# Recurrent layer: the four gates in three PSUM banks, two separate products, and the next chunk's normalisation one step later

## What is computed

```
x_proj = x @ W_ih.T + b_ih + b_hh
for every step t:
    gates = x_proj[t] + h @ W_hh.T
    i, f, g, o = split(gates, 4)
    c = sigmoid(f) * c + sigmoid(i) * tanh(g)
    h = sigmoid(o) * tanh(c)
```

## Time and profile before

| | us |
|---|---|
| median of 3 runs | 5656.29 (5656.06 to 5662.14) |
| the profiled execution's own time | 5652.6 |
| its span | 5650.8 |
| first step of the recurrent layer (AB) | at 4040.4 |
| last HT of the recurrent layer | at 5552.3 |
| VectorE's and the stores' tail behind it | 98 |
| TensorE busy, whole span | 4365.2 (77%) |
| VectorE busy, whole span | 3937.5 (70%) |
| ScalarE busy, whole span | 2516.5 (45%) |
| raw input transfer, issue to landing, median | 1.8 |

### The profile page before, as it was taken

One profiled execution on the slowest core, in us unless ns is written; L12 is line 12 of the kernel. 1 busy time (PEld: TensorE's weight loads), 2 busy tenths in 40 slices (PEclk: granted clock), 3 DMA queues, 4 the chain that ended last, 5 costly groups with the idle time before them and its releaser, 6 DMA issues. The chain is left out here.

```text
span 5650.8 us, 151689 instructions
## 1 busy us (share of the span) xinstructions
PE 4365.2 (77%) x55153; PEld 2972.8 (53%) x55295; DVE 3937.5 (70%) x9254; ACT 2516.5 (45%) x6434; POOL 1642.0 (29%) x1316
## 2 busy tenths in 40 slices
PE   6887888884888888888888868888487777777772
PEld 3444444442455555555555556666376666666662
DVE  5887888783777777777777758888365555555555
ACT  4666666662454555555455524444132323233330
POOL 4767676762223232332323211111000000000000
PEclk9999999996899999999999979999799999999996
DMA  2111111111000000000000023332211111111105
GB/s 58 46 60 46 60 45 60 50 52 41 16 16 21 17 19 19 19 19 15 22 15 19 16 71 105 105 104 93 49 26 26 26 26 24 27 24 27 26 23 124
DMA packets 322638, 233.54 MB, mean 41 GB/s; under 512 B 170381, under 2 KB 288525, under 8 KB 322061
## 3 DMA queue, kind: packets, MB, share of 16 engines
q1 hardware_dynamic: 288268, 217.37, 13.2%
q10 hardware_dynamic: 33792, 8.39, 0.7%
HBM read 158.55 MB, written 67.11 MB: 40 GB/s over the span
## 5 line engine op out<-in xcount | busy, mean ns | idle before, releaser
L2181 PE MATMUL lstm_G_psum<-lstm_Whh,lstm_HT 128*32 128x192 f32 x8192 | 447.2, 336 | 324.4 <-DVE lstm_HT L2353 281.4
L1398 PE MATMUL ssm_J_psum<-ssm_XT,ssm_W_in 128*128 128x512 f32 x1152 | 589.8, 637 | 104.0 <-DVE ssm_CV L1806 102.5
L538 ACT ACTIVATE g_relu<-g_Z_psum 128x512 f32<-128x512 f32 x640 | 380.2, 594 | 598.9 <-PE g_Z_psum L420 598.7
L706 DVE CUSTOM_DVE_ANT_0 g_S<-g_Z_psum,g_relu 128x512 f32<-128x512 f32 x640 | 437.8, 684 | 247.2 <-ACT g_relu L538 237.2
L427 PE MATMUL g_PT_psum<-g_ident,g_PR 128*128 128x128 f32 x2560 | 401.8, 280 | 239.7 <-DVE g_PT L714 164.0
L427 PEld LDWEIGHTS g_PT_psum<-g_ident,g_PR 128*128 128x128 f32 x2560 | 303.5, 143 | 439.2 <-issue 171.3
L547 ACT ACTIVATE g_PR<-g_S,g_nmax 128x512 f32<-128x512 f32 x640 | 460.0, 719 | 107.7 <-DVE g_nmax L706 103.2
L2247 ACT ACTIVATE lstm_TC<-lstm_G_psum 128x192 f32<-128x192 f32 x512 | 170.2, 332 | 749.3 <-PE lstm_G_psum L2181 749.3
L2173 PE MATMUL lstm_G_psum<-lstm_Wih,lstm_XT 128*32 128x192 f32 x8192 | 434.9, 330 | 0.0
L2476 POOL TENSOR_SCALAR lstm_rstd<-lstm_mv 128x4 f32<-128x4 f32 x32 | 7.2, 226 | 1470.2 <-DVE lstm_mv L2336 1470.2
L2181 PEld LDWEIGHTS lstm_G_psum<-lstm_Whh,lstm_HT 128*32 128x32 f32 x8192 | 216.9, 110 | 412.4 <-DVE lstm_HT L2353 333.8
(11 more groups left out here) (256 smaller groups left out, 10550.3 us busy)
## 6 DMA issues: line engine op xcount, KB each, us to landing
g_ADJ<-in_adj SPq DMA_DIRECT2D x64, 1024.0 KB, 6.1
x<-g_XO SPq DMA_DIRECT2D x64, 512.0 KB, 3.4
g_X<-in_x SPq DMA_DIRECT2D x32, 512.0 KB, 5.9
ssm_X<-x SPq DMA_DIRECT2D x32, 512.0 KB, 3.8
x<-ssm_OUT SPq DMA_DIRECT2D x32, 512.0 KB, 2.8
g_X<-x SPq DMA_DIRECT2D x32, 512.0 KB, 3.9
lstm_raw<-x SPq DMA_DIRECT2D x1024, 16.0 KB, 1.8
lstm_U<-x SPq DMA_DIRECT2D x128, 128.0 KB, 3.3
```

The lines of the kernel that those rows point to most:

```text
L538: act.activation(relu[n % 4][:, :], Zb[n % 2][:, :], ACT.Relu, scale=(1.0 - ALPHA) / ALPHA).then_inc(s["relu"], 1)
L706: v.tensor_tensor_reduce(S[n % 4][:, :], Zb[n % 2][:, :], relu[n % 4][:, :], -1.0, 3e38, ALU.add, ALU.min, nmax[:, n % 4:n % 4 + 1]).then_ ...
L1398: ins = pe.matmul(Jb[k % 2][:, :], W_in[:, kc, c:c + P], XT[:, kc, :], start=(kc == 0), stop=(kc == KC - 1))
L2181: ins = pe.matmul(bank[32 * j:32 * (j + 1), 0:last - first], HT[t % 2][:, 32 * kc:32 * (kc + 1)], Whh[:, kc, j, first:last], start=False, ...
```

## The change

Gates move from two pairs of banks to four banks: Gb[0] and Gb[1] hold i and g (128 columns), Fb holds f, Ob holds o, the last two without a second buffer. The weights and the bias are laid out in the order i, g, f, o (PLACE). ScalarE takes three tanh per step (i and g; f; o). VectorE computes IG = (i + 1) * g and FC = (f + 1) * c in two instructions of 64 elements and the cell goes to a tile of its own. The waits for the tiles' and banks' readers follow that. ScalarE's normalisation of the next chunk stands behind `cell` in steps 9 and 10 instead of 8 and 9. In VectorE's side work the second half's four passes go from steps 12 to 15 to steps 13 to 16, step 16 being step 0 of the chunk after.

```diff
+    PLACE = (0, 2, 1, 3)
...
-        TC = [m.sb(f"TC{k}", [P, 4, HB]) for k in range(2)]
+        TIG = [m.sb(f"TIG{k}", [P, 2, HB]) for k in range(2)]
+        TF = [m.sb(f"TF{k}", [P, HB]) for k in range(2)]
+        C = [m.sb(f"C{k}", [P, HB]) for k in range(2)]
...
-        AB = m.sb("AB", [P, 2, HB])
+        IG = m.sb("IG", [P, HB])
+        FC = m.sb("FC", [P, HB])
...
-        Ob = [m.ps(f"O{k}") for k in range(2)]
+        Fb = m.ps("F")
+        Ob = m.ps("O")
...
             def inputs(c, t):
...
-                for bank, first, last, read in ((Gb[t % 2], 0, IFG, s["tg"]), (Ob[t % 2], IFG, 4 * HB, s["to"])):
-                    c.wait(pe, read, S, t - 1)
+                for bank, first, last, read, back in ((Gb[t % 2], 0, 2 * HB, s["tg"], 2), (Fb, 2 * HB, 3 * HB, s["tf"], 1),
+                                                      (Ob, 3 * HB, 4 * HB, s["to"], 1)):
+                    c.wait(pe, read, S, t + 1 - back)
...
             def hidden(c, t):
                 c.wait(pe, s["ht"], S, t + 1)
-                for bank, first, last, made in ((Gb[t % 2], 0, IFG, s["g"]), (Ob[t % 2], IFG, 4 * HB, s["go"])):
+                for bank, first, last, made in ((Gb[t % 2], 0, 2 * HB, s["g"]), (Fb, 2 * HB, 3 * HB, s["gf"]),
+                                                (Ob, 3 * HB, 4 * HB, s["go"])):
...
             def gates(c, t):
                 c.wait(act, s["g"], S, t + 1)
-                c.wait(act, s["ab"], S, t - 1)
-                act.activation(TC[t % 2][:, 0:3, :].rearrange("p g e -> p (g e)"), Gb[t % 2][:, 0:IFG], ACT.Tanh
+                c.wait(act, s["ig"], S, t - 1)
+                act.activation(TIG[t % 2][:, :, :].rearrange("p g e -> p (g e)"), Gb[t % 2][:, 0:2 * HB], ACT.Tanh
                                ).then_inc(s["tg"], 1)
+                c.wait(act, s["gf"], S, t + 1)
+                c.wait(act, s["fc"], S, t - 1)
+                act.activation(TF[t % 2][:, :], Fb[:, 0:HB], ACT.Tanh).then_inc(s["tf"], 1)
+
+            def output_gate(c, t):
                 c.wait(act, s["go"], S, t + 1)
                 c.wait(act, s["h"], S, t - 1)
-                act.activation(TO[t % 2][:, :], Ob[t % 2][:, 0:HB], ACT.Tanh).then_inc(s["to"], 1)
+                act.activation(TO[t % 2][:, :], Ob[:, 0:HB], ACT.Tanh).then_inc(s["to"], 1)
...
                     gates(c, t)
+                    output_gate(c, t)
                     cell(c, t)
-                    if nxt and t in (8, 9):
-                        normalised(c + 1, 2 * (t - 8))
-                        normalised(c + 1, 2 * (t - 8) + 1)
+                    if nxt and t in (9, 10):
+                        normalised(c + 1, 2 * (t - 9))
+                        normalised(c + 1, 2 * (t - 9) + 1)
...
             def step(c, t):
                 c.wait(v, s["tg"], S, t + 1)
                 c.wait(v, s["c2"], S, t)
-                v.scalar_tensor_tensor(out=AB[:, :, :], in0=TC[t % 2][:, 0:2, :], scalar=1.0, in1=TC[t % 2][:, 2:4, :],
-                                       op0=ALU.add, op1=ALU.mult).then_inc(s["ab"], 1)
-                c.wait(v, s["ab"], S, t + 1)
-                v.scalar_tensor_tensor(out=TC[(t + 1) % 2][:, 3, :], in0=AB[:, 1, :], scalar=0.5, in1=AB[:, 0, :],
+                v.scalar_tensor_tensor(out=IG[:, :], in0=TIG[t % 2][:, 0, :], scalar=1.0, in1=TIG[t % 2][:, 1, :],
+                                       op0=ALU.add, op1=ALU.mult).then_inc(s["ig"], 1)
+                c.wait(v, s["tf"], S, t + 1)
+                v.scalar_tensor_tensor(out=FC[:, :], in0=TF[t % 2][:, :], scalar=1.0, in1=C[t % 2][:, :],
+                                       op0=ALU.add, op1=ALU.mult).then_inc(s["fc"], 1)
+                c.wait(v, s["fc"], S, t + 1)
+                v.scalar_tensor_tensor(out=C[(t + 1) % 2][:, :], in0=FC[:, :], scalar=0.5, in1=IG[:, :],
                                        op0=ALU.mult, op1=ALU.add).then_inc(s["c2"], 1)
...
                 if t == 12:
                     counted(c, 14)
                     counted(c, 15)
+                if t == 13:
                     before_it(c, 1)
-                if t == 13:
+                if t == 14:
                     before_added(c, 1)
-                if t == 14:
+                if t == 15:
                     up_to_it(c, 1)
-                if t == 15:
+                if t == S:
                     up_to_taken(c, 1)
...
                     step(c, t)
+                    if prev2 and t == 0:
+                        beside(c + -2, S)
```

More of the change, by code:

```diff
@@ L2015, in lstm_phase @@
     HALF = S // 2
-    IFG = 3 * HB
+    PLACE = (0, 2, 1, 3)
     with ExitStack() as ctx:
@@ L2055, in lstm_phase @@
         REP_AT = 2 * S
-        names = ("w setup_v setup_pe wready zero raw_in st mv rstd shift0 shift xn xt_pe xt g go tg to ab c2 tc h ht lgp lg "
+        names = ("w setup_v setup_pe wready zero raw_in st mv rstd shift0 shift xn xt_pe xt g gf go tg tf to ig fc c2 tc h ht lgp lg "
                  "gate repp gs inc part u done tot bias1 bias2 fin outs").split()
@@ L2245, in gates @@
                 c.wait(act, s["g"], S, t + 1)
-                c.wait(act, s["ab"], S, t - 1)
-                act.activation(TC[t % 2][:, 0:3, :].rearrange("p g e -> p (g e)"), Gb[t % 2][:, 0:IFG], ACT.Tanh
+                c.wait(act, s["ig"], S, t - 1)
+                act.activation(TIG[t % 2][:, :, :].rearrange("p g e -> p (g e)"), Gb[t % 2][:, 0:2 * HB], ACT.Tanh
                                ).then_inc(s["tg"], 1)
+                c.wait(act, s["gf"], S, t + 1)
+                c.wait(act, s["fc"], S, t - 1)
+                act.activation(TF[t % 2][:, :], Fb[:, 0:HB], ACT.Tanh).then_inc(s["tf"], 1)
+            def output_gate(c, t):
                 c.wait(act, s["go"], S, t + 1)
                 c.wait(act, s["h"], S, t - 1)
-                act.activation(TO[t % 2][:, :], Ob[t % 2][:, 0:HB], ACT.Tanh).then_inc(s["to"], 1)
+                act.activation(TO[t % 2][:, :], Ob[:, 0:HB], ACT.Tanh).then_inc(s["to"], 1)
             def cell(c, t):
                 c.wait(act, s["c2"], S, t + 1)
-                act.activation(tc[:, :], TC[(t + 1) % 2][:, 3, :], ACT.Tanh, scale=0.5).then_inc(s["tc"], 1)
+                act.activation(tc[:, :], C[(t + 1) % 2][:, :], ACT.Tanh, scale=0.5).then_inc(s["tc"], 1)
             def before(c):
@@ L2285, in _ @@
             v.memset(gate[:, :], 0.0)
-            v.memset(TC[0][:, 3, :], 0.0)
+            v.memset(C[0][:, :], 0.0)
             v.memset(inc[:, S, :], 0.0).then_inc(s["tot"], 1)
@@ L2296, in _ @@
                             scale = (1.0 if g == 2 else 0.5) * (0.5 if which else 1.0)
-                            v.tensor_scalar(W[:, c, 2 * (r % 2):2 * (r % 2) + 2, g * HB:(g + 1) * HB],
+                            at = PLACE[g] * HB
+                            v.tensor_scalar(W[:, c, 2 * (r % 2):2 * (r % 2) + 2, at:at + HB],
                                             XTb[n % 2][:, (r % 4) * P:(r % 4 + 1) * P].rearrange("p (j e) -> p j e", j=2),
@@ L2306, in _ @@
             for r in range(4):
-                v.tensor_scalar(b1.rearrange("p (j g e) -> p j g e", j=J, g=4)[:, :, r],
+                v.tensor_scalar(b1.rearrange("p (j g e) -> p j g e", j=J, g=4)[:, :, PLACE[r]],
                                 b3[:, r * D:(r + 1) * D].rearrange("p (j e) -> p j e", j=J),
@@ L2449, in body @@
                 nxt, prev = some or c.off < CH - 1, some or c.off > 0
+                prev2 = some or c.off > 1
                 for t in range(S):
                     step(c, t)
+                    if prev2 and t == 0:
+                        beside(c + -2, S)
                     if prev:
@@ L2457, in after @@
             def after(c):
-                for t in range(S):
+                beside(c + -1, S)
+                for t in range(S + 1):
                     beside(c, t)
```

## The result

The changed kernel takes 5918.48 us (median of 4 runs, 5910.87 to 5924.97) against 5657.08; the ratio is 1.046, interval 1.0442 to 1.0478. It is slower by 261 us where I forecast 93 us less. All of it lies in the recurrent layer: from the first HT to the last it took 1510.6 us and now takes 1771.5, 260.9 more. The mean step, from one HT to the next, went from 2.96 to 3.47 us.

A forecast was written before the change was run, and what follows sets the result against it. The prediction took a chain of waits, not an engine, to bound the recurrent layer's steady stretch. Its terms, -92 - 32 + 7 + 15 + 5 + 4 = -93 us, took 5656.3 to 5563 us, range 5545 to 5583.

The forecast's parts named there:

- TensorE's own length: TensorE's work per recurrent step: 76 pairs become 112 with the same columns, ending at 2.3 of 2.61 us.
- Rival D: TensorE's pairs cost by the instruction when sustained: 112 pairs take 3.0 us a step, total 5726 us; chance 0.05.
- The chain, 0.18 a step: Recurrent step's chain of waits: splitting the gates shortens each step by 0.18 to 2.61 us, -92 us over 512 steps.
- rival A: VectorE in the recurrent step: FC waits out IG, so the split gives only 0.10 a step, 5604 us; chance 0.13.
- The normalisation, -32: ScalarE's normalisation one step later: its wait for GpSimd's shift goes, 1.13 us in each of 28 chunks, -32 us.
- The turned steps, +7: Two steps per chunk where TensorE also transposes the next chunk's input: 0.11 lost in each of 62, +7 us.
- The late load, +15: SyncE's input load starts a step later, takes 23.2 us with instruction pages between, and lands 0.9 late: +15 us.
- Jumps, +5: The 13 loop-jump steps, set by TensorE: the 0.18 is not gained and the jump comes some 0.2 later, +5 us.

The follow-up runs named there:

- the bfloat16 run written out: Changed kernel with input products in bfloat16 and the recurrent layer's chunks written out without a loop: 5515.2 us, ratio 0.975.
- the bfloat16 run: Changed kernel with the input products in bfloat16, one pair instead of two each, loop kept: 5598.16 us, ratio 0.99.

## Why the prediction was wrong

**The failed step** is "TensorE's own length": "Per step 76 pairs of weight load and product become 112. Columns are the same", and from it "TensorE then ends at 2.3 of 2.61", resting on "columns count, not instructions". As work, the 2.3 came out: in the step above, from 4218.18 to the end of its logit products at 4220.77, less the stop, TensorE works 2.31 us, and it still executes sixteen pairs in 0.22 us (the f group, 4218.64 to the o group at 4218.86). What fails is the term that the prediction put at nothing: the time to bring these instructions to TensorE. The runs put in its place: 256 instructions per 3.7 to 3.8 us, weight loads and products of every width used here. The changed kernel asks for a page in 3.0 us of chain (256 of 224 in 2.63) and gets one in 3.74. The numbers to see it stood in the prediction. It counted 235 instructions to a page and 0.365 pages a us for the new pace, one in 2.74 us, and spent that only on SyncE's issues. It never asked whether TensorE could have a page in 2.74 us. Its own sign of being wrong altogether, an ordinary step outside 2.58 to 2.70, was there to see: 3.325 in the mean. No row of before shows the limit, since the need there was one in 4.56 us in the mean; the jump row, 3.2 us for a first page, was the nearest, and a bound from it would have given 2.8 us a step (224 of 256), above the chain's 2.61.

**Rival D** named the side and the place, though its price was 192 us short: a cost per pair when sustained, deciding from 23 ns a pair, 27 ns taken, 5726 us, chance 0.05. Measured, a pair costs two instructions of 14.6 ns, 29 ns, at the steady pace: 112 of them are 3.3 us, which is the step seen. On top come the jump steps, 6.15 us before and 8.89 now, 13 x 2.74 = 36 us of the 261. The other 225 are 498 steps at 3.325 in place of 2.873. The mechanism was not the engine's pace per pair, as D had it, but the list's supply. The totals do not tell the two apart, since both grow with the pairs; the trace does. A pace of its own would keep TensorE at work all the time, but it works 2.3 us a step, which is 21 ns a pair and below D's 23, and stands the rest in one piece every 256 instructions. In the run with 36 pairs in one column group something like D did happen: there the work alone passes the chain.

**The Trainium skill** ("TensorE: Matmul & The Clock Gate", Back-to-back issue gap) speaks of about 25 ns for small products. I set it aside on the burst's 14 ns, rightly for products spread over the four column groups. In one column group the run with 36 more pairs has just its 25 ns. The 29 ns measured as a sustained figure lie near it by chance, since they come from the pages. The other rule ("Runtime: NRT & Kernel Launch", Instruction fetch mechanics) calls a page's crossing mostly hidden. The traces agree down to one page in 3.86 us (the bfloat16 run written out, mean step 2.68) and contradict it where a list asks for more.

**The chain, 0.18 a step:** right, 2.62 to 2.63 for 2.61, visible in the kernels that are not starved. FC did overlap IG by 0.06, so rival A fell.

**The normalisation, -32:** right alone (-29), worth nothing here (5913.79 against 5918.48).

**The turned steps, +7:** too dear. In the bfloat16 run, whose TensorE is shorter, and in the one without f and o inputs, the steps from 11 to 13 take 2.63 in the median. For TensorE's full length it was not seen, as no such kernel is unstarved.

**The late load, +15:** the mechanism is there, the size not. In the loop of the bfloat16 run a load takes 21.8 us in the mean in place of 19.8 (forecast 23.2 in place of 19.55). The cost of a page on SyncE was too low, 1.0 us and not 0.87, and the pages too many, one in 3.75 us came and not one in 2.74. Two of its loads (order of time, SyncE):

```profile
4569.10 21.93 SPq L2120 DMA_DIRECT2D lstm_raw<-x  x32
4611.24 22.41 SPq L2120 DMA_DIRECT2D lstm_raw<-x  x32
```

and VectorE waits for it once in 1100 us, 0.2 us: there the margin was just enough.

**Jumps, +5:** +36. At a jump TensorE stands 4.8 us in place of 3.3 (means of 13; the longest 5.0 and 3.6), and at ten jumps out of ten in 1100 us two pages' transfers lie 0.3 to 0.9 us apart. The rest of the 2.74 us a jump was not taken apart.

## What to carry to other kernels

Count the instructions of TensorE's list per microsecond of the new chain, not only its columns. Here 256 instructions per 3.7 us was the ceiling (14.5 ns each, pairs count twice, float32 products four times), and small products in column groups of 32 reach it easily. Where a chain is shortened by splitting products, first find what pays for the added ones: a cheaper type, or work left out. An "issue" stop inside a group of equal instructions, at 256 from the last, is this limit; a loop's jump asks for it too, and writing the loop out shortened the whole by 6.4 us per jump with bfloat16 inputs, by 8.5 in the changed kernel (its other steps shortened too; the jump steps alone give 5.6) and by 3.3 in the other. Put added instructions that are to test such a limit where they cost the engine no work of its own, or count that work first.

## What the hardware showed that I had not expected

- One page at a time: transfer 1.1 us, but 3.67 to 3.83 us from page to page in the mean of 1100 us in the seven runs that stand for pages again and again (300 pages without bias, 298 in the changed kernel written out, 287 with 36 more pairs). Single pages came down to 3.3 us apart. Transfers that start less than 3 us apart occur in none of the three runs without jumps in the recurrent layer.
- A page's transfer holds up the issue of other transfers on SyncE's queue by 1.0 us: the load of 32 small transfers would take 15.8 us undisturbed (an estimate from the usual 0.50 us between two issues), and takes 19.8 with one page in 4.6 us and 21.8 with one in 3.75.
- One whole-array weight load among 32-column ones costs TensorE some 0.2 us more than the four small ones that it replaces (three a step: 2.88 us of work in place of 2.3).
- Pairs of weight load and two-column product in one column group follow each other every 25 ns, pairs spread over four column groups every 14 ns.
- Where pages were the bound, a removed wait of 1 us a chunk did not show in the time (5918 against 5914 us). What a shorter chain is worth there, no pair of runs separates.
